# Queries and keys in three blocks of 128 channels, an earlier root on POOL, and two smaller edits, in a vision tower layer on one core

## What is computed

```python
h = tok(x, W, b, gamma, beta)                     # patch embedding (5 shifted images) and layer norm
h = concatenate([cls_tok, h])                     # 16 images x 37 tokens x 192 channels = 592 tokens
h = h + attn(layernorm(h))                        # 12 heads of 16 channels
#   s = q k^T; s = einsum('bhnm,hg->bgnm', s, w_l) + b_l; p = softmax(s)
#   p = einsum('bhnm,hg->bgnm', p, w_w) + b_w;  out = (p v) w_proj + b_proj
h = h + ffn(layernorm(h))                         # 8 experts 192 -> 512 -> 192, silu, best 2 of 8 per token
#   probs = softmax(h @ router_w.T); importance = probs.sum(axis=0)
#   running = 1 + 0.1 * (importance - 1) + 0.01
#   weight of a chosen expert = probs / running, scaled so that the two add up to 1
```

## Time and profile before

| | us |
|---|---|
| runs | 157.54, 158.01, 158.03 |
| median | 158.01 |
| profiled execution | 158.57 |
| its span, first to last instruction | 156.4 |
| PE / PEld / DVE / ACT / POOL busy | 143.7 / 122.1 / 93.0 / 73.3 / 81.3 |

### The profile page before, as it was taken

The page is one execution under the profiler, slowest core; times in us unless marked ns, Lnnn a source line. Parts: engine busy times, 40 slices in busy tenths (PEclk is TensorE's granted clock), DMA queues, the critical chain, the costliest instruction groups (busy, mean ns, idle before and its releaser), DMA issues.

```text
span 156.4 us, 3122 instructions
## 1 busy us (share of the span) xinstructions
PE 143.7 (92%) x1010; PEld 122.1 (78%) x1010; DVE 93.0 (59%) x260; ACT 73.3 (47%) x158; POOL 81.3 (52%) x121
## 2 busy tenths in 40 slices
PE   0589969999999999999999799999999999999992
PEld 0467959669658575755878499899999999999991
DVE  6666496799999799989978574211121111342183
ACT  8997253655842326898814762032332322323210
POOL 7000282049999729999968872433433334437300
PEclk9999999999999999999999999999999999999999
DMA  5999993131179925569999122899866666500523
GB/s 200 383 388 411 257 266 80 48 91 44 40 258 402 419 87 174 171 179 276 257 407 351 46 80 57 211 248 265 207 175 170 158 173 185 154 16 2 152 81 116
DMA packets 16529, 30.04 MB, mean 192 GB/s; under 512 B 2775, under 2 KB 11210, under 8 KB 16514
## 3 DMA queue, kind: packets, MB, share of 16 engines
q1 hardware_dynamic: 14737, 27.80, 57.5%
q0 software_dynamic: 1216, 1.83, 3.8%
q10 hardware_dynamic: 562, 0.23, 0.6%
HBM read 21.98 MB, written 8.34 MB: 194 GB/s over the span
## 4 chain that ended last, share of the span: by engine, by line
PE 47%; DVE 19%; POOL 17%; issue 7%; DMA 5%; SPq 2%; ACT 1%; POOLq 0%; DVEq 0%
PE ps L1351 20%; PE ps L1370 14%; POOL vw L458 10%; DMA early<-in_patches 5%; DVE early L766 4%; PE ps L1385 3%; POOL xrows L471 3%; PE ps L1073 3%; PE ps L1116 3%; PE ps L1338 2%; DVE mx L813 2%; POOL ve L429 2%; DVE h L752 2%; DVE prob L816 1%; DVE sm L823 1%
## 5 line engine op out<-in xcount | busy, mean ns | idle before, releaser
L458 POOL TENSOR_TENSOR vw<-v,wm 111x384 f32<-111x384 f32 x32 | 32.9, 1057 | 7.7 <-DMA v<-vrows 7.7
L1351 PE MATMUL ps<-early,w1r 128*128 128x128 f32 x272 | 33.0, 275 | 0.3 <-issue 0.2
L1351 PEld LDWEIGHTS ps<-early,w1r 128*128 128x128 f32 x272 | 32.2, 192 | 0.6 <-DVE early L1057 0.3
L1057 DVE COPY early<-ps 96x256 f32<-96x256 f32 x15 | 6.3, 422 | 36.5 <-PE ps L1338 36.5
L548 POOL DMA_INDIRECT yrows<-early,sid x14 | 13.8, 984 | 25.6 <-ACT early L708 24.3
L1370 PE MATMUL ps<-early 128*128 (+1 forms) x136 | 24.8, 327 | 0.0
L702 ACT ACTIVATE early<-ps 128x512 f32<-128x512 f32 x17 | 10.2, 599 | 25.4 <-PE ps L1351 25.4
L1370 PEld LDWEIGHTS ps<-early 128*128 128x128 f32 x136 | 21.8, 190 | 0.0
L1073 PE MATMUL ps<-wsum,early 128*128 128x192 f32 x32 | 11.2, 521 | 6.7 <-DVE wsum L737 6.6
L1073 PEld LDWEIGHTS ps<-wsum,early 128*128 128x128 f32 x32 | 9.1, 315 | 8.5 <-issue 8.5
L598 ACT ACTIVATE early<-qk,wls 96x74 f32<-96x74 f32 (+1 forms) x48 | 14.3, 378 | 0.1
(11 more groups left out here) (150 smaller groups left out, 237.1 us busy)
## 6 DMA issues: line engine op xcount, KB each, us to landing
w1r<-in_w SPq DMA_DIRECT2D x17, 384.0 KB, 4.2
xrows<-zero SPq DMA_DIRECT2D x1, 4053.0 KB, 14.0
early<-in_w SPq DMA_DIRECT2D x4, 768.0 KB, 12.5
early<-in_patches SPq DMA_DIRECT2D x5, 608.0 KB, 6.4
early<-xrows SPq DMA_DIRECT2D x17, 96.5 KB, 3.0
spare<-in_pixels SPq DMA_DIRECT2D x3, 512.0 KB, 12.7
yrows<-zero SPq DMA_DIRECT2D x1, 960.0 KB, 4.7
v<-vrows SPq DMA_DIRECT2D x12, 72.0 KB
```

Source lines behind the costliest of these rows:

```text
L458: nc.gpsimd.tensor_tensor(vw[0:CHK, j % VWS, a, q:q + PART, :], v3[:, 2 * j + a, :].unsqueeze(1).to_broadcast([CHK, PART, C]), wm[:, q:q + ...
L1351: m = nc.tensor.matmul(ps[:, s % 2, P * i:P * i + P], w1r[:, s % RING, c, P * i:P * i + P], xgt[:, s % 3, c, :], start=(c == 0), stop=(c = ...
```

## The change

1. The columns of w_qkv are ordered so that three blocks of 128 hold queries 0 to 127, keys 0 to 127, and the last 64 channels of the queries (partitions 0 to 63) together with the last 64 of the keys (64 to 127). `queries_keys` has six matmuls instead of eight. ACT takes them out with two copies: three blocks by 128 partitions, and the 64 queries of the third block once more into a fourth. Part c=0 of `ks` has 128 partitions, part c=1 has 64; the c=1 keys are read from partitions 64 to 127 and written to 0 to 63. Ones, zeros and bias move to part 1, from partition 64 on.
2. `root2(4)` stands ahead of `scatter(2, (0,))`, right behind `root2(3)`.
3. DVE adds up the probabilities of tiles 0 to 3 (`pr_sum`), so that `importance` is two matmuls instead of five.
4. Half 0 of `gather` uses 128 weight columns instead of 96 and writes 128 partitions, of which 96 are used.

```diff
@@ @block.gpsimd
             root2(3)
-            scatter(2, (0,))
             root2(4)
-            scatter(2, (1,))
+            scatter(2)
             scatter(3)
             scatter(4)
@@ @block.scalar
-            clear(qk[HC:P, 0:2, :], score_pads_set)
+            nc.scalar.activation(qk[REST:P, 3, :], ones[REST:P, 0:1].to_broadcast([P - REST, TP]), ACT.Copy, scale=0.0).then_inc(score_pads_set, 1)
...
+            act.wait_ge(score_pads_set, 3)
+            nc.scalar.dma_start(ks[REST:REST + 1, 1, :, :].rearrange("p b n -> p (b n)"), bias_l).then_inc(ld_bl, 16)
...
             def queries_keys_out(i):
                 act.wait_ge(qk_ps, i + 1)
-                nc.scalar.activation(qk[0:HC, :, P * i:P * i + P], ps[0:HC, 6, :].rearrange("p (n t) -> p n t", n=4),
-                                     ACT.Copy).then_inc(qk_ready, 1)
+                nc.scalar.activation(qk[:, 0:3, P * i:P * i + P], ps[:, 6, 0:3 * P].rearrange("p (n t) -> p n t", n=3), ACT.Copy)
+                nc.scalar.activation(qk[0:REST, 3, P * i:P * i + P], ps[0:REST, 6, 2 * P:3 * P], ACT.Copy).then_inc(qk_ready, 1)
@@ @block.vector
             def keys(j, c):
 
+                lo = 0 if c == 0 else REST
                 dve.wait_ge(qk_ready, (74 * j + 73) // P + 1)
                 nc.vector.tensor_tensor(
-                    ks[0:HC, c, 2 * j:2 * j + 2, :].rearrange("p a (g m) -> p a g m", g=HEADS),
+                    ks[0:P - lo, c, 2 * j:2 * j + 2, :].rearrange("p a (g m) -> p a g m", g=HEADS),
...
+                    qk[lo:P, 1 + c, 2 * j * TOK:2 * (j + 1) * TOK].rearrange("p (a m) -> p a m", a=2).unsqueeze(2).to_broadcast([P - lo, 2, HEADS, TOK]),
+                    wls[lo:P, c, :].unsqueeze(1).unsqueeze(3).to_broadcast([P - lo, 2, HEADS, TOK]), ALU.mult).then_inc(ks_pair, 1)
...
+            dve.wait_ge(pr_ready, 1)
+            nc.vector.reduce_sum(pr_sum[:, :], pr[:, 0:TILES - 1, :].rearrange("p i e -> p e i"), AX.X).then_inc(pr_summed, 1)
             dve.wait_ge(counts_ps, 1)
@@ @block.tensor
-                for n in range(4):
+                for n in range(3):
                     for c in range(2):
-                        m = nc.tensor.matmul(ps[:, 6, P * n:P * n + P], wqkv[:, c, HC * n:HC * n + P],
+                        m = nc.tensor.matmul(ps[:, 6, P * n:P * n + P], wqkv[:, c, P * n:P * n + P],
...
-                        m = nc.tensor.matmul(ps[64 * a:64 * a + 64, j % 2, 0:GM], qk[:, c, img * TOK:img * TOK + 64],
+                        m = nc.tensor.matmul(ps[64 * a:64 * a + 64, j % 2, 0:GM], qk[:, 3 * c, img * TOK:img * TOK + 64],
...
-                    m = nc.tensor.matmul(ps[0:HC, c, 0:GATHERED * P], xid[0:n, i, 0, HC * c:HC * c + HC],
+                    m = nc.tensor.matmul(ps[0:P if c == 0 else HC, c, 0:GATHERED * P], xid[0:n, i, 0, HC * c:P if c == 0 else C],
...
             def importance():
-                pe.wait_ge(pr_ready, 1)
-                for i in range(TILES):
-                    n = P if i < TILES - 1 else TAIL
-                    m = nc.tensor.matmul(ps[:, 7, 0:EXPERTS], ones[0:n, :], pr[0:n, i, :], start=(i == 0), stop=(i == TILES - 1))
-                m.then_inc(imp_ps, 1)
+                pe.wait_ge(pr_summed, 1)
+                nc.tensor.matmul(ps[:, 7, 0:EXPERTS], ones[:, :], pr_sum[:, :], start=True, stop=False)
+                nc.tensor.matmul(ps[:, 7, 0:EXPERTS], ones[0:TAIL, :], pr[0:TAIL, TILES - 1, :], start=False, stop=True).then_inc(imp_ps, 1)
```

More of the change, by code:

```diff
@@ L24 @@
 HC = C // 2
+REST = C - P
 HEADS = 12
@@ L130, in build @@
         wqkv = sb("wqkv", [P, 2, 3 * C + EXPERTS])
-        wl = sb("wl", [HC, 2, HEADS])
+        wl = sb("wl", [P, 2, HEADS])
         wm = sb("wm", [CHK, GQ, C])
@@ L153, in build @@
         wsum = sb("wsum", [P, KC, C])
-        wls = sb("wls", [HC, 2, HEADS])
+        wls = sb("wls", [P, 2, HEADS])
         h = sb("h", [P, TILES, C])
@@ L185, in build @@
         pr = sb("pr", [P, TILES, EXPERTS])
+        pr_sum = sb("pr_sum", [P, EXPERTS])
         top = sb("top", [P, TILES, 8])
@@ L288, in build @@
         pr_ready = sem("pr_ready")
+        pr_summed = sem("pr_summed")
         m_ready = sem("m_ready")
@@ L569, in _ @@
             clear(wo[HC:P, :, :], out_pad_set)
-            clear(qk[HC:P, 0:2, :], score_pads_set)
+            nc.scalar.activation(qk[REST:P, 3, :], ones[REST:P, 0:1].to_broadcast([P - REST, TP]), ACT.Copy, scale=0.0).then_inc(score_pads_set, 1)
             act.wait_ge(score_pads_set, 1)
-            nc.scalar.activation(qk[HC:HC + 1, 0, :], ones[HC:HC + 1, 0:1].to_broadcast([1, TP]), ACT.Copy).then_inc(score_pads_set, 1)
-            clear(early[HC:P, CHUNK_AT[-1]:], score_pads_set)
+            nc.scalar.activation(qk[REST:REST + 1, 3, :], ones[REST:REST + 1, 0:1].to_broadcast([1, TP]), ACT.Copy).then_inc(score_pads_set, 1)
+            rest_of = 2 * IMAGES * GM - CHUNK_AT[-1]
+            nc.scalar.activation(early[REST:P, CHUNK_AT[-1]:], ones[REST:P, 0:1].to_broadcast([P - REST, rest_of]), ACT.Copy, scale=0.0).then_inc(score_pads_set, 1)
             clear(pt[HC:P, :, :, :], mix_pads_set)
@@ L593, in queries_keys_out @@
                 act.wait_ge(qk_ps, i + 1)
-                nc.scalar.activation(qk[0:HC, :, P * i:P * i + P], ps[0:HC, 6, :].rearrange("p (n t) -> p n t", n=4),
-                                     ACT.Copy).then_inc(qk_ready, 1)
+                nc.scalar.activation(qk[:, 0:3, P * i:P * i + P], ps[:, 6, 0:3 * P].rearrange("p (n t) -> p n t", n=3), ACT.Copy)
+                nc.scalar.activation(qk[0:REST, 3, P * i:P * i + P], ps[0:REST, 6, 2 * P:3 * P], ACT.Copy).then_inc(qk_ready, 1)
             def scale_keys(c, g, a, z):
                 nc.scalar.activation(
-                    ks[0:HC, c, a:z, g * TOK:(g + 1) * TOK], qk[0:HC, 2 + c, a * TOK:z * TOK].rearrange("p (b m) -> p b m", m=TOK),
-                    ACT.Copy, scale=wls[:, c, g:g + 1]).then_inc(ks_act, 1)
+                    ks[0:P if c == 0 else REST, c, a:z, g * TOK:(g + 1) * TOK],
+                    qk[0 if c == 0 else REST:P, 1 + c, a * TOK:z * TOK].rearrange("p (b m) -> p b m", m=TOK),
+                    ACT.Copy, scale=wls[0 if c == 0 else REST:P, c, g:g + 1]).then_inc(ks_act, 1)
             def normal(i):
@@ L1484 @@
     w_w = f(L0_attn_w_w)
+    packed = np.concatenate([np.arange(P), C + np.arange(P), np.arange(P, C), C + np.arange(P, C), np.arange(2 * C, 3 * C)])
+    mix_l = np.repeat(f(L0_attn_w_l), DH, axis=0)
     arrays = {
@@ L1487 @@
         "gamma": np.broadcast_to(f(L0_tok_gamma), (P, C)), "base": base, "ident": np.eye(P, dtype=np.float32),
-        "w_in": halves(f(L0_attn_w_qkv), f(L0_attn_b_qkv)),
-        "mix_l": halves(np.repeat(f(L0_attn_w_l), DH, axis=0)),
+        "w_in": halves(f(L0_attn_w_qkv)[:, packed], f(L0_attn_b_qkv)[packed]),
+        "mix_l": np.stack([mix_l[:P], np.concatenate([np.zeros((REST, HEADS), np.float32), mix_l[P:]])], axis=1),
         "bias_l": np.tile(np.repeat(f(L0_attn_b_l), TOK), IMAGES)[None],
```

3 lines of the change are left out of this document (removed).

## The result

| | before | after |
|---|---|---|
| median of 20 executions, us | 158.06 | 159.69 |
| ratio, 95% interval | | 1.0063 (1.0034 to 1.0092) |
| profiled execution / its span, us | 158.57 / 156.4 | 160.29 / 157.8 |
| PE / PEld / DVE / ACT / POOL busy, us | 143.7 / 122.1 / 93.0 / 73.3 / 81.3 | 141.7 / 120.1 / 93.2 / 73.3 / 81.3 |
| granted clock, mean over the span | 1.000 | 0.989 |

The forecast was 157.7 us, in a range up to 158.6, and "slower" had a chance of 0.17. It was slower, by more than the range holds. PE is busy for 2 us less and the end comes later.

A forecast was written before the change was run, and what follows sets the result against it. POOL's path, fed by DVE before 58.8 us, was taken to set the end, with PE's savings lost in waiting. Terms -0.84 + 0.54 + 0.05 = -0.25, about 0.3 us off the 158.01 median, gave 157.7 us; range 156.9 to 158.6.

The forecast's parts named there:

- the pricing of edit 2: Last root moved ahead of a scatter: +0.05 us on POOL's path, gather(4) on PE some 1.3 us earlier.
- slot 2 arrives near 98.0: Ahead of slot 2, PE is ready near 96.1 and idles 1.5 to 2 us until the transfer through DRAM.
- -0.84 + 0.14 forecast: DVE's third `keys`: 0.84 us earlier as its idle time goes, 0.14 later for partition changes at tile 0.
- +0.40 for the holds behind it: DVE before 58.8 us: four further changes of partition in `keys`, 0.10 us each, add 0.40 us.
- rival B: No holds on DVE from changes of partition: the whole 0.84 us arrives, 157.2 us; chance 0.28.
- hangs on a POOL root and not on PE: DVE's second `keys` waits for POOL's root, so it ends at 28.04 us both before and after.
- Rival D: DVE and POOL block each other, up to 0.9 us a time: 158.0, chance 0.12, or 157.0, chance 0.05.
- Rival C: The moved root waits for tile 4's variance ahead of six scatters, delaying them: slower, 158.7 us; chance 0.13.
- forecast 0.61: Sum of the probabilities: ten PE records in 1.02 us become four in 0.41, saving PE 0.61 us.
- The sum of my terms: On POOL's path -0.84 + 0.54 + 0.05 = -0.25 us plus a few hundredths; the end moves by 0.3 us.

The follow-up runs named there:

- `again`: The changed kernel with no edit, run once more against the kernel before: 157.59 us, ratio 0.9959.
- `swap`: The changed kernel with keys first and queries second in the third block, so keys on DVE read from partition 0: 160.06 us, ratio 1.0143.
- `again3`: The changed kernel with no edit, in a later session against the kernel before: 158.38 us, ratio 1.0035.
- `again2`: The changed kernel with no edit, in another session against the kernel before: 159.61 us, ratio 1.0079.
- `fill`: The changed kernel with eight transposes of the identity on PE between narrow(1) and the turning of slot 2: 159.58 us, ratio 1.0095.

## Why the prediction was wrong

**The step that failed** is the pricing of edit 2: "What is gained is on PE", costed at +0.05 us on POOL's path, with "slot 2 arrives near 98.0, PE stands idle there for 1.5 to 2 us, and the saved PE work is turned into that wait". I took an earlier PE to cost nothing. Without holding that is right: `again` waits 0.99 + 0.32 us there, and half a microsecond of filler changes nothing. With holding the earlier widen(0) doesn't bring an earlier silu; ACT gets it 2.2 us behind the last scatter's start, narrow(0) starts 2.9 us behind it instead of 1.9 in both profiles of the kernel before, and with 2.6 us or more of narrow that outlasts the transfer. So the 5.48 us from the last scatter to widen(2) become 6.44, and 8.2 where the clock falls behind the idle time; the prediction had no term for the clock either. No rival had a signal of PE arriving late, and the one profile at hand showed none. The cause of the late signals stays open.

**A second missed term** is "Outside the span lie 2.17 us", which I carried over unchanged: +0.29 us with edit 2, undone by one wait instruction.

**Keys and queries: each hold right in size, the sum within the scatter.** -0.84 + 0.14 forecast, -0.68 measured to the first maximum; +0.40 for the holds behind it, +0.31 measured in this pair, each change 0.11 us where I took 0.10. The rule of the Trainium skill (page "VectorE: DVE Perf Modes", section "Two Vector instructions with no wait between them") is that an instruction whose input or output begins in another group of 32 partitions than the last one read or written starts only when all earlier ones have finished. The trace agrees, by 0.11 us a change, and rival B, which had no holds, is out.

One reading of the single profile was too narrow: that the second `keys` "hangs on a POOL root and not on PE". In five of the seven profiles without edit 1 DVE waits 0.51 to 0.66 us for ACT's copy ahead of the first `keys`, so a part of edit 1's gain lies ahead of it, where the table's first row is. From PE's first record of queries to the first maximum it is 5.82 or 5.83 us in ten of the twelve profiles with edit 1 (`swap` left out), and 6.64 to 6.72 in all seven without. From that record to POOL's root the means are 35.00 and 35.34 us, so behind all holds about 0.3 us is left, and single profiles differ by more.

**Rival D was real**, behind POOL's root and not ahead of it: +0.24 us between root and first scatter in all thirteen profiles with edit 1 (20.62 to 20.66, against 20.36 to 20.41 in all seven without), `swap` without holds included. I had it at 0.12 with a mishap of either sign; here it was no matter of luck, it came every time, and it takes back most of the 0.3 us that edit 1 gains. From first `keys` to POOL's root the profiles scatter more: 32.16 to 32.83 us in the two of the kernel before, 31.59 to 33.61 in the four of the changed one.

**The rest.** Rival C didn't happen (84.77 against 84.92). Edit 3 saved PE 0.67 us (from 1.18 for the ten records to 0.51 for the four, forecast 0.61). Edit 4 can't be told from none; no run had it alone. The sum of my terms, without holding, was -0.3 us: `again` and `again3` gave -0.7 and 0.0 against their medians of before: sessions differ by more than the term itself.

## What to carry to other kernels

An engine that becomes early is not free: look at what it signals to, and whether the one that waits for that signal has slack if it comes late. Cut two traces at the same instructions and take the differences of the stretches before reading any single wait. Read more than one profile of both kernels, from the same session and from different ones, before a change of half a per cent is called understood. Compare what lies outside the span too: a term of 0.3 us sat there.

## What was unexpected of the hardware

- In some sessions PE's semaphore signals reached ACT and DVE up to 3.6 us after the matmul's recorded end while POOL's scatters ran, in others within 0.02 us, with the same kernel; one chip gave both. Ends of matmuls are modelled, so that the matmuls themselves ran late, and not their signals, isn't excluded. In the same profiles the trace lacks 51 to 59 of its entries on semaphores, so that the recording has a part in it isn't excluded either.
- With the early root the late signals come at nearly the same point in every profile of a holding session: 2.16 to 2.23 us behind the start of the last scatter, which is 3.55 to 3.60 us behind widen(0)'s end in the five without a shift.
- In four of these six profiles the granted clock fell to 0.50 during narrow(0), behind 1.4 to 2.1 us of idle PE; in `again2` and `fill` it didn't, behind 2.1 us, nor in `again`, behind 1.3 us in two pieces (there it fell at 19.5 us). So idle time ahead of narrow goes with the fall and doesn't decide it. Of the executions with the early root, 22 of 46 in holding sessions had a mean granted clock below 0.995 (wherever in the span it fell), 19 of 114 in the others; of the kernel before, 17 of 44 and 37 of 99.
- One wait instruction less on POOL made the time outside the span 0.26 us longer, behind the last instruction.
